# GpSimd normalises the rows itself, the second statistics are spread, and row transfers and the last quad's values change place

## The reference, cut to what matters

```python
def reference(x, qkv_w, proj_w, proj_b, curvature, ..., expert_weights, expert_indices, w1, w2, bias):
    # x: (8, 1024, 256); 16 heads of 16; causal everywhere
    # heads 0-5 dot-product, heads 6-9 hyperbolic (arccosh distance), heads 10-15 cosine attention
    x = _layernorm(x + attention(x) @ proj_w.T + proj_b)     # (v - mean) / sqrt(var + 1e-5) over 256
    x = _layernorm(x + experts(x) + bias)                    # top 2 of 8 experts, for batch 0's 1024 tokens
    return x
```

## Time and profile before

| | us |
|---|---|
| three runs | 2302.31, 2297.95, 2299.3 |
| median | 2299.3 |
| the profiled execution: time / span | 2287.28 / 2285.4 |

### The profile page before, as it was taken

The page is one execution under the profiler, slowest core; times in us unless marked ns, Lnnn a source line. Parts: engine busy times, 40 slices in busy tenths (PEclk is TensorE's granted clock), DMA queues, the critical chain, the costliest instruction groups (busy, mean ns, idle before and its releaser), DMA issues. The chain is left out here.

```text
span 2285.4 us, 40063 instructions
## 1 busy us (share of the span) xinstructions
PE 1799.4 (79%) x13330; PEld 960.5 (42%) x13330; DVE 1355.4 (59%) x3184; ACT 1417.4 (62%) x1400; POOL 714.8 (31%) x404
## 2 busy tenths in 40 slices
PE   6888888843887886896897797897788689646994
PEld 3344443421333443442443343443344344235894
DVE  4777676763654765765776585576576576550103
ACT  2333333322889887887888888888788788711110
POOL 0000000000434544544544544444454465520002
PEclk9999999976988997997998998998899799778997
DMA  5222233328044044125305405504404420109972
GB/s 192 89 106 107 110 111 111 111 100 167 11 76 67 11 67 116 26 38 105 66 8 96 105 2 94 106 10 85 113 11 68 111 51 25 52 35 353 352 277 67
DMA packets 88454, 217.45 MB, mean 95 GB/s; under 512 B 14112, under 2 KB 34848, under 8 KB 83936
## 3 DMA queue, kind: packets, MB, share of 16 engines
q1 hardware_dynamic: 79840, 184.74, 31.1%
q0 software_dynamic: 8448, 30.41, 4.2%
HBM read 146.52 MB, written 68.58 MB: 94 GB/s over the span
## 5 line engine op out<-in xcount | busy, mean ns | idle before, releaser
L1065 ACT ACTIVATE a_PT<-a_s 128x1024 f32<-128x1024 f32 (+3 forms) x576 | 459.6, 809 | 181.0 <-PE a_s L885 108.5
L882 PE MATMUL a_s<-a_Q,a_K 96*128 96x512 bf16 (+7 forms) x1152 | 335.7, 356 | 123.6 <-ACT a_PT L1065 78.0
L1261 DVE TENSOR_REDUCE a_mx<-a_w 128x1 f32<-128x512 f32 (+2 forms) x576 | 308.0, 551 | 55.3 <-PE a_w L910 42.3
L1143 POOL TENSOR_TENSOR a_Z<-a_Z,a_R 128x2182 f32<-128x2182 f32 x64 | 290.4, 4537 | 144.3 <-ACT a_R L1077 144.2
L897 PE MATMUL a_o<-a_PT,a_V 128*32 128x512 f32 (+3 forms) x2304 | 269.9, 543 | 77.8 <-ACT a_PT L1065 47.5
L1140 POOL TENSOR_TENSOR a_R<-a_Z 128x2182 f32<-128x2182 f32 x64 | 245.0, 3828 | 259.8 <-DVE a_Z L1253 196.7
L1253 DVE TENSOR_SCALAR_CACHE_REDUCE a_Z<-a_w 128x512 f32<-128x512 f32 (+7 forms) x384 | 202.6, 529 | 146.5 <-PE a_w L925 101.9
L245 PE MATMUL p_ps<-p_xT,p_w 128*128 128x512 f32 x512 | 243.6, 635 | 44.7 <-ACT p_xT L341 23.8
L942 PE MATMUL a_w<-a_ident,a_R 128*128 128x128 f32 (+1 forms) x1152 | 209.1, 309 | 24.9 <-POOL a_R L1150 13.8
L1307 DVE COPY a_PTh<-a_w 128x512 f32<-128x512 f32 (+1 forms) x256 | 157.7, 621 | 112.1 <-PE a_w L942 108.7
L910 PE MATMUL a_w<-a_K,a_Q 96*128 96x512 bf16 (+2 forms) x576 | 187.6, 333 | 34.5 <-DVE a_mx L1261 11.4
(11 more groups left out here) (161 smaller groups left out, 2799.7 us busy)
## 6 DMA issues: line engine op xcount, KB each, us to landing
e_w<-in_w SPq DMA_DIRECT2D x23, 2048.0 KB, 9.1
qk_parts<-p_parts SPq DMA_DIRECT2D x32, 768.0 KB, 3.5
a_Q<-qk_parts SPq DMA_DIRECT2D x144, 128.0 KB, 5.3
a_K<-qk_parts SPq DMA_DIRECT2D x144, 128.0 KB, 7.6
v_rows<-p_vt SPq DMA_DIRECT2D x8, 2048.0 KB, 7.7
a_V<-v_rows SPq DMA_DIRECT2D x32, 512.0 KB, 8.7
p_xin<-in_x SPq DMA_DIRECT2D x8, 1024.0 KB, 6.7
a_X<-in_x POOLq DMA_DIRECT2D x8, 1024.0 KB, 8.2
```

What stands on the lines that cost most here:

```text
L882: m = pe.matmul(sB[x % 2][:, i, 0:w], Kb[0:r, h, P * j:P * j + P], Qb[0:r, h, t0:t0 + w], start=True, stop=not diag)
L1065: act.activation(PT[:, u % 2, 2 * k:2 * k + 2, 0:w], sB[x % 2][:, :, 0:w], ACT.Exp, scale=scale_of(GROUPS[g][2 * k])).then_inc(prob.sem, 1)
L1143: pool.tensor_tensor(z, z, r, ALU.add).then_inc(z_sum.sem, 1)
L1261: dve.tensor_reduce(mx[:, pc, col:col + 1], wB[x % WB][:, 0:w], AX.X, ALU.max).then_inc(wide_free.sem, 1)
```

## The change

- GpSimd does the normalising itself: 8 `tensor_scalar` instructions of 128 x 256 in one item, directly behind `newton` (slots 112 and 130), in place of VectorE's two halves.
- `newton` takes five small steps: GpSimd adds the 1e-5 itself. ScalarE reads the variance directly, with 1e-5 as the activation's bias, and so no longer waits for VectorE's addition.
- The second statistics stand in four slots (122 to 125), two row tiles in each; `variance` 1 moves from 125 to 126, `inverse_root` 0 from 106 to 107, `inverse_root` 1 from 126 to 128, `newton` 1 from 129 to 130.
- `rows_out` moves from 133 to 136 (behind `square` 7), `rows_in` from 141 to 143 (behind `add_root` 7).
- The last quad's values move into slot 2 of the next turn and its sums into slot 3, each now put before the units' items of that slot; `turn_sums` 5, 6 and 7 move one slot back. The 37th step is gone.
- In the tail the values of the last quad are one of the wrapped items, and the normalising is one item.

```diff
-        work = [[[] for _ in range(NSLOT)] for _ in range(NQ + 1)]
+        work = [[[] for _ in range(NSLOT)] for _ in range(NQ)]
...
-        for u in range(1, NQ + 1):
-            work[u][VALUES if u < NQ else 0].append(("values", u - 1))
-            if (u - 1) % 12 in (3, 11):
-                work[u][VALUES + 1 if u < NQ else 0].append(("sums", 2 * ((u - 1) // 12) + ((u - 1) % 12 == 11)))
...
+        for u in range(1, NQ + 1):
+            put(u * NSLOT + VALUES, ("values", u - 1))
+            if (u - 1) % 12 in (3, 11):
+                put(u * NSLOT + VALUES + 1, ("sums", 2 * ((u - 1) // 12) + ((u - 1) % 12 == 11)))
...
-        SUMS = {0: 119, 1: 123, 2: 143, 5: 149, 6: 153, 7: 157, 3: 178, 4: 181}
+        SUMS = {0: 119, 1: 123, 2: 143, 5: 150, 6: 154, 7: 158, 3: 178, 4: 181}
...
-        for at, item in ((25, ("shift",)), (104, ("variance", 0)), (106, ("inverse_root", 0)),
-                         (112, ("newton", 0)), (114, ("normalize", 0, 0)), (115, ("normalize", 0, 1)), (116, ("mid_out",)),
-                         (121, ("add_bias",)), (123, ("statistics", 1, 0, NT // 2)), (124, ("statistics", 1, NT // 2, NT)),
-                         (125, ("variance", 1)), (126, ("inverse_root", 1)), (129, ("newton", 1)),
-                         (131, ("normalize", 1, 0)), (132, ("normalize", 1, 1)), (133, ("rows_out",)), (141, ("rows_in",))):
+        for at, item in ((25, ("shift",)), (104, ("variance", 0)), (107, ("inverse_root", 0)), (112, ("newton", 0)),
+                         (112, ("normalize", 0)), (116, ("mid_out",)), (121, ("add_bias",)),
+                         (122, ("statistics", 1, 0, 2)), (123, ("statistics", 1, 2, 4)), (124, ("statistics", 1, 4, 6)),
+                         (125, ("statistics", 1, 6, 8)), (126, ("variance", 1)), (128, ("inverse_root", 1)),
+                         (130, ("newton", 1)), (130, ("normalize", 1)), (136, ("rows_out",)), (143, ("rows_in",))):
...
             def inverse_root(d, a):
-                act.wait_ge(var_ready.sem, var_ready.at(d, a))
-                act.activation(rs[:, 1], rs[:, 0], ACT.Ln).then_inc(rs_ln.sem, 1)
+                act.wait_ge(stats.sem, stats.at(d, 2 * NT * (a + 1) - 1))
+                act.activation(rs[:, 1], mv[:, :, 1], ACT.Ln, bias=tiny[:]).then_inc(rs_ln.sem, 1)
...
+                    hold(pool, rs_exp.sem, rs_exp.at(d, n), pool_passed)
+                    step(0, pool.tensor_scalar(rs[:, 0], mv[:, :, 1], 1e-5, None, ALU.add))
+                    step(1, pool.tensor_tensor(rs[:, 2], rs[:, 0], rs[:, 1], ALU.mult))
+                    step(2, pool.tensor_tensor(rs[:, 2], rs[:, 2], rs[:, 1], ALU.mult))
+                    step(3, pool.tensor_scalar(rs[:, 2], rs[:, 2], -0.5, 1.5, ALU.mult, ALU.add))
+                    step(4, pool.tensor_tensor(rs[:, 1], rs[:, 1], rs[:, 2], ALU.mult))
+                elif kind == "normalize":
+
+                    for t in range(NT):
+                        ins = pool.tensor_scalar(X[:, t, :], X[:, t, :], mv[:, t, 0:1], rs[:, 1, t:t + 1],
+                                                 ALU.subtract, ALU.mult)
+                    ins.then_inc(normed.sem, 1)
...
-                    dve.wait_ge(stats.sem, stats.at(d, 2 * NT * (a + 1) - 1))
-                    dve.tensor_scalar(rs[:, 0], mv[:, :, 1], 1e-5, None, ALU.add).then_inc(var_ready.sem, 1)
-                elif kind == "normalize":
-                    _, a, part = item
-                    if part == 0:
-                        dve.wait_ge(rs_step.sem, rs_step.at(d, 4 * a + 3))
-                    for n in range(NT // 2 * part, NT // 2 * (part + 1)):
-                        ins = dve.tensor_scalar(X[:, n, :], X[:, n, :], mv[:, n, 0:1], rs[:, 1, n:n + 1],
-                                                ALU.subtract, ALU.mult)
-                    if part:
-                        ins.then_inc(normed.sem, 1)
```

More of the change, by code:

```diff
@@ L719, in attend @@
             tail += [("turn_rows", n + 1)] * (n + 1 < NT) + [("project", n), ("statistics", 0, n, n + 1)]
-        tail += [("variance", 0), ("inverse_root", 0), ("newton", 0), ("normalize", 0, 0), ("normalize", 0, 1), ("mid_out",),
+        tail += [("variance", 0), ("inverse_root", 0), ("newton", 0), ("normalize", 0), ("mid_out",),
                  ("add_bias",), ("statistics", 1, 0, NT), ("variance", 1), ("inverse_root", 1), ("newton", 1),
-                 ("normalize", 1, 0), ("normalize", 1, 1), ("rows_out",)]
+                 ("normalize", 1), ("rows_out",)]
         tail_wide = {item: x for x, item in enumerate([it for it in tail if it[0] in RINGED])}
@@ L1105, in turn @@
                     for k, slot in enumerate(step):
-                        if u < NQ and k % 2 == 0:
+                        if k % 2 == 0:
                             exponentials(b, u, k // 2)
@@ L1156, in do @@
                 elif kind == "newton":
-                    pool.wait_ge(rs_exp.sem, rs_exp.at(d, n))
                     def step(k, ins):
                         ins.then_inc(rs_step.sem, 1)
-                        pool.wait_ge(rs_step.sem, rs_step.at(d, 4 * n + k))
-                    step(0, pool.tensor_tensor(rs[:, 2], rs[:, 0], rs[:, 1], ALU.mult))
-                    step(1, pool.tensor_tensor(rs[:, 2], rs[:, 2], rs[:, 1], ALU.mult))
-                    pool.sem_inc(pool_passed, 1)
-                    step(2, pool.tensor_scalar(rs[:, 2], rs[:, 2], -0.5, 1.5, ALU.mult, ALU.add))
-                    step(3, pool.tensor_tensor(rs[:, 1], rs[:, 1], rs[:, 2], ALU.mult))
-                    pool.sem_inc(pool_passed, 1)
+                        hold(pool, rs_step.sem, rs_step.at(d, 5 * n + k), pool_passed)
+                    hold(pool, rs_exp.sem, rs_exp.at(d, n), pool_passed)
[9 more added lines that the diff above has]
+                    ins.then_inc(normed.sem, 1)
                 elif kind == "shift":
```

25 lines of the change are left out of this document (13 added, 12 removed).

## The result

The changed kernel takes 2340.4 us (median of four runs, 2337.7 to 2342.9) where the kernel before takes 2300.6: ratio 1.0174, 95% interval 1.0155 to 1.0193. It is 40 us slower; 2280.8 was forecast, with a range of 2255 to 2305. The execution profiled has a span of 2341.2 us, that of before 2285.4, which is the fastest execution of before on record here. The rest is 21 us in the turns and 25 in the tail, less 2 behind it.

The account below looks back on a forecast made before the run. Engines waiting for each other, neither PE nor ACT full, were taken to set the turn. Gains 7 x 3.65 = 25.5 and 3, losses 6 (clock) and 4 (tail): 18.5 us off 2299.3 gives 2280.8 us, range 2255 to 2305.

Parts of the forecast that it names:

- the price of one instruction on GpSimd: One normalising instruction of 256 columns on GpSimd was taken at 0.45 us, bounds 0.41 and 0.75, 3.6 us for eight.
- a sign of being wrong: Wrong if PE's wait before the first `argument` product were absent, or if a GpSimd instruction took 0.75 us.
- the overlap built on it: Normalising on GpSimd behind `newton`: `mid_out` goes out at 864.9 in place of 867.37, 2.5 us sooner per turn.
- The slower rival: GpSimd's normalising holds its queue: at 1.0 us per instruction `mid_out` comes 2.0 us later, 2321 us; chance 0.12.
- Spreading the statistics: Second statistics over more slots let the clamps through sooner, counted as nothing; the 1e-5 addition leaving VectorE gains 0.65 us.
- the second idle time: PE's 2.74 us before an `argument` product, released by a clamp behind VectorE's statistics and addition of 1e-5.
- The turn's end: Between slot 132 and the next turn's slot 4, row transfers and last quad gain 0.5 us at each of six ends.
- SP's chain: SP's 24 load transfers from 888.00 end last before the next turn's first `argument` product; PE waits 4 to 5 us there.
- The first turn's length: The first turn end has no row work, so nothing is gained there and the length stays unchanged.
- The clock: A stretch at granted clock 0.50 behind PE's moved wait at every turn end: 1.0 us lost, bounds 0 and 3.4.
- The tail: After the last turn: `shift` waits for `rows_in`, 3 us, normalisings and `newton` 1 us; 4 us lost, bounds 0 and 10.
- The collision: VectorE's four normalising instructions beside GpSimd's `square` take 4.88 us, where four take 1.38 us elsewhere.

Follow-up runs that it names:

- the fastest version: Changed kernel with VectorE normalising in slots 112, 113, 130, 131, last statistics earlier, tail's shift behind the wrapped items: 2234.6 us, ratio 0.9722 against the kernel before.

## Why the prediction was wrong, step by step

| part | alone, against before | forecast |
|---|---|---|
| GpSimd normalises | +2.11%, +48 us | gain of 2.5 us a turn, tail +1 |
| statistics spread, 1e-5 off VectorE | -0.75%, -17 us | 0.65 us a turn |
| row transfers | +0.46%, +11 us | with the last quad 0.5 us a turn, tail +3 |
| last quad's values | +0.27%, +6 us | with the row transfers |
| sum / the change | +48 / +40 us | -18.5 us |

Each part's ratio is uncertain by 4 to 8 us, so the sum and the change do not contradict each other.

*The step that failed is the price of one instruction on GpSimd*: "I take 0.45 us", with 0.41 and 0.75 as bounds, measured 1.22. It was 0.47 us above the upper bound, and by the prediction's own words an instruction of 0.75 us was a sign of being wrong. The bounds came from a copy and from an addition of two tensors, and the sentence "it reads one tensor, like the copy, but works on it twice" treated the form as harmless. As the form decides the price by a factor of three, rows of other forms bounded nothing. With it fell the overlap built on it: `mid_out` was to go out 2.5 us sooner than before, and VectorE's wait for its transfer to stay as long; it goes out 3.5 us later behind `newton`, and the wait is 10.17 us in place of 3.83. The slower rival had the mechanism right, with "none of the simple instructions of GpSimd is that slow" against it: `mid_out` later, and VectorE's wait for the transfer longer in every turn. Its own formula with the measured price: 4.5 us a turn at 1.0 us, 8 x 0.22 = 1.8 more at 1.22, so 44 us in seven turns; 16 x (1.22 - 0.45) = 12 in the tail; 2280.8 + 44 + 12 = 2337 us, against 2340.4. Its mechanism is what the runs show; that the number comes so near is partly luck. The 2280.8 that it starts from counts some 10 us too little for the statistics, and some 10 us too little loss for the row transfers and the last quad, and these two errors cancel. Its chance, 0.12, was too small.

*Spreading the statistics* was counted as nothing, and only the addition, 0.65 us, on the path. The two together bring 17 / 7 = 2.4 us a turn. The sentence that the spreading "lets the clamps through sooner" was the right reading of the second idle time; giving it zero was not. Which of the two edits brings how much was not tried apart.

*The turn's end.* That SP's chain "ends last" there was half right. With the last quad moved alone, PE does stand 3.4 us before its first `argument` product for the small loads; but with fewer loads the wait goes and nothing is gained, for PE waits for the masks instead. The expectation of such a wait at every turn end of the changed kernel, 4 to 5 us, was wrong: its list of waits has 2.9 us behind the turns.

```profile
PE a_w L927 <- DMA a_K<-t_parts: 24.3, 4, 21.4
```

SP's issuing is the same in both kernels: its last issue ends 14.9 to 16.0 us after the last `argument` product. But where the product waits for the loads it starts 1.8 to 6.6 us after that issue with the last quad moved alone, and 1.8 to 3.3 in the changed kernel. So the landing was sized too narrowly, at 1.4 to 2.0 us; why it varies stays open. The first turn's length, "unchanged", does not hold: it is 170.5 to 173.5 us in the eight other kernels profiled with the last quad moved, 174.2 to 179.3 in the five without; only in the one profile of after it is 176.9.

*The clock.* One low stretch more per turn was allowed for, 1.0 us. PE's busy time of a turn went from 150.96 us at a granted clock of 0.92 to 153.39 at 0.91, 2.4 us more, and in the fastest version to 146.84.

*The tail.* The tail was forecast as 4 us longer, bounds 0 and 10, and 3 of them were the shift's. The row transfers alone cost 8.0 and putting the shift behind the masks gives 8.2 back. The two normalisings were given 1 us; GpSimd's 9.66 in place of 2.7 make 2 x 7 = 14, and with VectorE normalising the changed kernel's tail is 14.6 us shorter (99.0). Measured 25.4 for the whole tail.

*The collision* was read rightly, and the cure was looked for in the wrong place. The prediction capped the gain at 2.5 us because VectorE would wait for the same transfer; in the fastest version this wait is 0.22 us, with `mid_out` going out ahead of `square` 6 and not behind it. The better remedy was two slots away on VectorE (`newton` three slots earlier, `mid_out` two), not on another engine.

## What to carry to other kernels

Before an operation is moved to another engine, its price there has to be known in the very form it will have (constants, per-partition columns, a second tensor); rows of neighbouring forms are no bounds. A collision between two engines can be taken away by moving one of the two a few slots; here such a move, which also put the transfer behind it ahead of the other engine's long instruction, gave 24 us, where the other engine cost 48. And when several chains end within a few microseconds of each other, as at this turn's end, removing the wait that the profile names only shows the next one: judge such an edit by the distance from turn to turn, as the last quad's values show: 6.30 us of idle time gone, nothing gained.

## What the runs showed of the hardware

GpSimd's prices for 128 x 256 values in f32: copy 0.39 us, multiply and add with two constants 0.40, second tensor 0.61, addition of one constant 0.86, one per-partition column 0.91, two of them 1.23. The Trainium skill, "GPSIMD Engine Reference", section "Engine selection", calls GpSimd's one-input work roughly line-rate. Beside VectorE's 0.35 us for the normalising, the copy and the two constants come near that; the addition of one constant does not, and with two per-partition columns GpSimd takes 3.5 times as long as VectorE.

Where two of these instructions collide, one stands for nearly the whole overlap, and it can be either side. VectorE's four normalisings began 0.24 us ahead of `square` 6, and while that ran its usual 3.85 us, they took 4.88 us in place of 1.38, 3.50 more, nearly the square's length. In the changed kernel VectorE's addition was under way (892.46 to 894.75) when `add_root` began at 893.04; the addition took its usual 2.29 us, and `add_root` 6.40 in place of 4.82, 1.58 more for an overlap of 1.71. The Trainium skill, "SBUF — State Buffer", section "Who interferes with whom", says of VectorE's two-port modes that whoever issues first gets the shared pair of ports for the whole instruction and the other fully blocks. The trace agrees instruction by instruction: of the four, the first takes 0.41 us, and the second, which starts 0.08 us behind `square` 6, takes 3.92 and ends 0.15 us after it. So a row of short instructions that began first still loses to a long one that starts between two of them.
